# Centred products with tokens on the partitions, squares with row sums on ScalarE

## The reference, cut to what matters

```python
def _ln(x, g, b):
    mu = jnp.mean(x, axis=-1, keepdims=True)
    var = jnp.mean(jnp.square(x - mu), axis=-1, keepdims=True)
    return (x - mu) * jax.lax.rsqrt(var + EPS) * g + b

x1 = jnp.einsum('btd,hd->bth', x, sw1) + sb1
x2 = jnp.einsum('btd,hd->bth', x, sw2) + sb2
sh = _ln(jax.nn.silu(x1) * x2, s_ln_g, s_ln_b)       # 128 hidden features
shared_out = jnp.einsum('bth,dh->btd', sh, sw3) + sb3
...                                                   # a router and 8 experts, of the same form,
                                                      # for up to 512 routed tokens
final_out = shared_out.at[index_b, index_t].set(shared_moe_out + expert_moe_out)
```

## Time and profile before

| | us |
|---|---|
| median of three runs | 607.18 (607.03 to 607.24) |
| the profiled execution | 604.62 |
| its span | 602.0 |
| TensorE (PE) busy | 567.1, 94% of the span |
| VectorE (DVE) busy | 409.0, 68% |
| ScalarE (ACT) busy | 264.3, 44% |
| the squares L499, 8 operations | 4.8 |
| the variance matmuls L612, 64 passes | 8.1 |
| the centring matmuls L604, 16 | 4.8 |

### The profile page before, as it was taken

How to read it: one execution, slowest core, us unless ns; L and a number is a source line. 1 busy time by engine, 2 the same in 40 slices (tenths; PEclk the granted TensorE clock), 3 DMA queues, 4 the chain that set the end, 5 groups by cost and what they waited for, 6 DMA issues and landing times.

```text
span 602.0 us, 17044 instructions
## 1 busy us (share of the span) xinstructions
PE 567.1 (94%) x5093; PEld 499.6 (83%) x5094; DVE 409.0 (68%) x1092; ACT 264.3 (44%) x577; POOL 178.1 (30%) x529
## 2 busy tenths in 40 slices
PE   5999999999999999999999999999999979999770
PEld 4888888876899999999999999989999958667650
DVE  4969977757565868685677888756474735686560
ACT  6666667532444434344334343434343425464320
POOL 0350000000763444443424244443434002870000
PEclk9999999999999999999999999999999979999895
DMA  8812345001001232310000000000000001922130
GB/s 272 261 46 71 105 141 170 23 1 36 2 1 38 106 107 106 107 71 3 3 2 3 1 4 1 4 2 3 1 3 4 2 4 59 359 76 71 48 129 9
DMA packets 28482, 36.93 MB, mean 61 GB/s; under 512 B 4762, under 2 KB 24115, under 8 KB 28132
## 3 DMA queue, kind: packets, MB, share of 16 engines
q1 hardware_dynamic: 28292, 35.57, 18.0%
q0 software_dynamic: 96, 0.20, 0.1%
HBM read 27.30 MB, written 8.53 MB: 60 GB/s over the span
## 4 chain that ended last, share of the span: by engine, by line
PE 91%; DVE 3%; issue 1%; ACT 1%; DMA 1%; SPq 1%; POOL 0%; POOLq 0%; DVEq 0%
PE ps_out L1180 40%; PE ps_hidden L1152 39%; PE ps_hidden L592 3%; PE ps_hidden L641 1%; PE ps_out L612 1%; DMA W<-in_xT 1%; PE ps_turn L625 1%; PE ps_small L625 1%; PE ps_out L1223 1%; DVE X L782 1%; PE ps_out L604 1%; DVE hbuf L1327 0%; PE ps_hidden L625 0%; SPq L970 0%; DVE W L1311 0%
## 5 line engine op out<-in xcount | busy, mean ns | idle before, releaser
L1180 PE MATMUL ps_out<-hbuf,W 128*128 128x242 f16 (+2 forms) x2304 | 250.7, 269 | 0.7 <-DVE W L1311 0.6
L1180 PEld LDWEIGHTS ps_out<-hbuf,W 128*128 (+1 forms) x2304 | 223.8, 98 | 21.0 <-issue 1.3
L1721 POOL COPY xs<-X 128x88 f16 x352 | 128.4, 414 | 287.0 <-PE ps_hidden L1152 175.1
L1022 ACT ACTIVATE h<-ps_hidden,b 128x242 f32<-128x242 f32 (+1 forms) x384 | 155.8, 467 | 79.8 <-PE ps_hidden L1152 78.0
L1152 PE MATMUL ps_hidden<-xs,W 128*128 128x242 f16 x1536 | 164.2, 267 | 0.8 <-issue 0.8
L1152 PEld LDWEIGHTS ps_hidden<-xs,W 128*128 x1536 | 149.4, 98 | 10.8 <-issue 1.6
L1327 DVE TENSOR_TENSOR hbuf<-h,hbuf 128x484 f16<-128x484 f32 (+2 forms) x192 | 129.9, 676 | 7.4
L1608 DVE SCALAR_TENSOR_TENSOR acc<-ytmp,wrow,acc 128x44 f32 (+1 forms) x352 | 65.8, 259 | 92.4 <-ACT ytmp L1113 88.0
L1152 PE MATMUL ps_hidden<-X,W 128*128 128x256 f16 (+1 forms) x768 | 92.7, 283 | 10.3 <-DVE W L1311 6.1
L1325 DVE CAST hbuf<-h 128x484 f16<-128x484 f32 (+2 forms) x192 | 84.7, 441 | 22.4 <-ACT h L1022 21.2
L1152 PEld LDWEIGHTS ps_hidden<-X,W 128*128 128x128 f16 x768 | 76.6, 100 | 23.5 <-DVE W L1311 5.8
(11 more groups left out here) (291 smaller groups left out, 297.3 us busy)
## 6 DMA issues: line engine op xcount, KB each, us to landing
stage<-in_ew SPq DMA_DIRECT2D x16, 512.0 KB, 3.7
stage<-in_xR SPq DMA_DIRECT2D x8, 512.0 KB, 3.8
moved_rows<-stage SPq DMA_DIRECT2D x8, 512.0 KB, 2.6
X<-moved_rows SPq DMA_DIRECT2D x8, 512.0 KB, 9.2
out_rows<-X SPq DMA_DIRECT2D x16, 256.0 KB, 2.2
W<-in_xT SPq DMA_DIRECT2D x7, 512.0 KB, 9.2
W<-in_fw SPq DMA_DIRECT2D x1, 2304.0 KB, 12.5
W<-in_sw SPq DMA_DIRECT2D x4, 256.0 KB, 3.3
```

What stands on the lines that cost most here:

```text
L1022: i = nc.scalar.activation(h32[:, j, k * size:(k + 1) * size], ps1[j][:, k * size:(k + 1) * size], ACT.Gelu_apprx_tanh, bias=b1[:, bass.ds ...
L1180: mm = pe.matmul(out, w2(e, wp, hb, db), h, start=(n == 0), stop=(n == 3 * HB - 1))
L1721: i = nc.gpsimd.tensor_copy(xs[:, parity, :, j * SEG:(j + 1) * SEG], X[:, :, bass.ds(cols[j], SEG)])
```

## The change

`centre(k)` uses g's halves as the weights and `Cm` as the moving operand, group by group: 8 matmuls of 128 columns for 2 of 512. `Cm` is symmetric, so the result is the same matrix turned over: tokens on the partitions, features along the free dimension. `square(k)` becomes four operations of 128 columns, each with a second output, `accum_out`, the sum of its row: a token's sum of squares, in `sums2`. `variance` and its semaphore `var_mm` go away. `centre` alternates between the banks `psy[0]` and `psy[1]` and waits for the square of two chunks before. `roots` and `late_roots_in` wait for `sq_ready` and read `sums2` in place of `psy[1]`; `turn_hot`, which writes `psy[1]`, waits for the last square.

```diff
         qms = stf[:, 876:876 + 2 * MG]
+        sums2 = stf[:, 884:884 + NQ * MG]
         ohT = stf[0:FE, 1024:1024 + P]
...
         s_ready, g_made, g_hi, g_ready = sem("s_ready"), sem("g_made"), sem("g_hi"), sem("g_ready")
-        c_done, sq_ready, var_mm = sem("c_done"), sem("sq_ready"), sem("var_mm")
+        c_done, sq_ready = sem("c_done"), sem("sq_ready")
         var_taken, gvar_taken = sem("var_taken"), sem("gvar_taken")
...
                 act.wait_ge(c_done, k + 1)
-                if k >= 2:
-                    act.wait_ge(var_mm, k - 1)
-                nc.scalar.activation(sq[:, k % 2, :], psy[0], ACT.Square).then_inc(sq_ready, 1)
+                for n in range(MG):
+                    i = nc.scalar.activation(sq[:, k % 2, n * P:(n + 1) * P], psy[k % 2][:, n * P:(n + 1) * P],
+                                             ACT.Square, accum_out=sums2[:, k * MG + n:k * MG + n + 1])
+                i.then_inc(sq_ready, 1)
 
...
                 pe.wait_ge(g_ready, k + 1)
-                if k >= 1:
-                    pe.wait_ge(sq_ready, k)
-                else:
+                if k >= 2:
+                    pe.wait_ge(sq_ready, k - 1)
+                elif k == 0:
                     pe.wait_ge(late_done, 2)
-                for part in range(2):
-                    mm = pe.matmul(psy[0], Cm, ghl[:, k % GR, part, :], start=(part == 0), stop=(part == 1))
+                for n in range(MG):
+                    for part in range(2):
+                        mm = pe.matmul(psy[k % 2][:, n * P:(n + 1) * P], ghl[:, k % GR, part, n * P:(n + 1) * P], Cm,
+                                       start=(part == 0), stop=(part == 1))
                 mm.then_inc(c_done, 1)
-
-            def variance(k):
-                pe.wait_ge(sq_ready, k + 1)
-                if k >= 2:
-                    pe.wait_ge(var_taken, k // 2)
-                for n in range(MG):
-                    mm = pe.matmul(psy[1][:, k * MG + n:k * MG + n + 1], sq[:, k % 2, n * P:(n + 1) * P],
-                                   onesm[:, 0:1], start=True, stop=True)
-                mm.then_inc(var_mm, 1)
 
...
                 pe.wait_ge(hot2_ready, g + 1)
-                pe.wait_ge(var_taken, NQ // 2)
+                pe.wait_ge(sq_ready, NQ)
                 pe.transpose(psy[1][0:FE, 0:P], roh, ident[:, :]).then_inc(hot_turned, 1)
...
                 centre(k - 1)
-                if k >= 2:
-                    variance(k - 2)
                 if k >= 4:
...
             centre(NQ - 1)
-            variance(NQ - 2)
             second(4)
-            variance(NQ - 1)
             second(5)
...
             def roots(q):
-                dve.wait_ge(var_mm, 2 * q + 2)
+                dve.wait_ge(sq_ready, 2 * q + 2)
                 two = slice(2 * q * MG, (2 * q + 2) * MG)
-                nc.vector.tensor_scalar(tms, psy[1][:, two], 1.0 / FH, EPS, ALU.mult, ALU.add).then_inc(var_taken, 1)
+                nc.vector.tensor_scalar(tms, sums2[:, two], 1.0 / FH, EPS, ALU.mult, ALU.add).then_inc(var_taken, 1)
                 dve.wait_ge(var_taken, q + 1)
...
             def late_roots_in(q):
-                dve.wait_ge(var_mm, 2 * q + 2)
+                dve.wait_ge(sq_ready, 2 * q + 2)
                 two = slice(2 * q * MG, (2 * q + 2) * MG)
-                nc.vector.tensor_scalar(tms, psy[1][:, two], WS * WS / FH, EPS * WS * WS, ALU.mult,
+                nc.vector.tensor_scalar(tms, sums2[:, two], WS * WS / FH, EPS * WS * WS, ALU.mult,
                                         ALU.add).then_inc(var_taken, 1)
```

## The result

| | us |
|---|---|
| kernel before, median | 607.21 (607.03 to 607.63, 4 runs) |
| changed kernel, median | 603.39 (602.18 to 604.04, 4 runs) |
| ratio | 0.9934, 95% interval 0.9917 to 0.9951 |
| predicted | 604.7 (602.5 to 607.6) |

The changed kernel is 3.8 us faster; 2.5 was forecast. Measured again beside 23 runs of the kernel before, the ratio was 0.9925 (0.9897 to 0.9953).

A forecast was written before the change was run, and what follows sets the result against it. TensorE, busy 94% of 602.0 us, was taken as the bound. Of 4.74 us removed 0.90 stays; with 0.11 at its return and 1.50 in the tail, 2.5 less: 604.7 us, range 602.5 to 607.6.

The forecast's parts named there:

- 4.74 us taken out: Six groups of variance matmuls on TensorE's chain ahead of 560.77, 0.79 us each; all but 0.90 was to be taken back.
- S: ScalarE's queue time for one chunk's four squares with row sums; taken as 1.6 us, bounds 0.8 and 2.1, far end 3.0.
- The 0.95 for the high half of the input: ScalarE's queue time in each chunk's round for the half of the sum, 0.95 us of a 3.67 us round.
- the sum is nearly free: Rival: ScalarE's row sums add little, squares take 0.8 to 1.2 us a chunk; gain 3.7 to 4.5, 602.6 to 603.5; chance 0.15.
- three signs: Forecast wrong if squares' queue time is under 1.2 or over 2, TensorE shows no centring gaps, or the tail's low clock goes.
- main case: Forecast's own case: ScalarE's squares take 1.2 to 1.95 us a chunk, weight loads hidden; 603.4 to 606.0 us; chance 0.46.
- The walk: Stepping three engine queues in order with trace durations through the loop over k; TensorE's return behind the gap 1.01 us earlier.
- Waits at the centrings and at second(1): New TensorE waits in the loop: 0.57, 0.62, 0.62, 0.30, 0.44 and 1.12, together 3.67 us.
- the forecast 1.4: VectorE's inverse roots at chunk 3 were to start 1.4 us later than before, 534.21 against 532.79.
- Centring at 57 ns a matmul: Eight TensorE matmuls of 128 columns with weight loads hidden, 0.46 us a centring, +0.03 over before.
- The tail: From TensorE's return to the routed tokens' first centring: 4.61 us for 6.11, two variance groups gone, a gain of 1.50.
- The base: Whole kernel: profiled execution 604.62 becomes 602.1; the runs' median, 2.6 above the profiled one, gives 604.7 us.

The follow-up runs named there:

- squares made twice: Changed kernel with each chunk's four squares and row sums made a second time into spare buffers nobody reads; 605.2 us, ratio 0.9971 to the kernel before.
- split squares in the kernel before: Kernel before with only ScalarE's square split into four operations of 128 columns with unused row sums; 609.6 us, ratio 1.0034.
- without sums: Changed kernel with the squares' row sums taken out and the sums set to a constant 1; 602.9 us, ratio 0.9930 to the kernel before.
- wide centring: Changed kernel with the centring as before, two matmuls of 512 columns with the constant as weight; 603.1 us, ratio 0.9946 to the kernel before.
- filled pair: Changed kernel and kernel before, with 28 and 36 useless matmuls in TensorE's gap behind the last centring; 600.2 and 604.8 us.

## Why the prediction was right, and where it was off

- **That the 4.74 us taken out would mostly turn into waits at ScalarE and VectorE: right in kind, too large in size.** The term mis-sized is S, the square's queue time with its sums: 1.02 for 1.6. A square of 128 columns takes 0.16 of the queue (0.21 was taken) and the reading 0.09 (0.20 was taken, on the premise that it overlaps nothing; it overlaps both neighbours). The 0.95 for the high half of the input was also a little small: its row ends 0.09 us before the square starts, not after, and in the changed kernel it holds the queue for 0.99. The case that came is the rival *the sum is nearly free*, S 0.8 to 1.2, with 602.6 to 603.5; it had 0.15, and the measured 603.4 is in it. By two of the prediction's own three signs its main case was wrong: S is under 1.2, and ahead of the centrings of chunks 1 to 3 TensorE shows no gaps. The number fell inside the range because the range took in this rival, and that it is no further from 604.7 is partly luck: the mis-sized S made the forecast gain too small by 1.7 us, and the second low stretch, which nobody foresaw, takes up to 2.4 us from the real one.
- **The walk was right.** With S = 1.02 in place of 1.6 and nothing else altered it gives, shifted by 0.82 us so that chunk 1's first layer starts where the changed trace has it: first layer of chunk 5 at 535.19, `second(1)` 540.11, the last of `gfirst` 556.91, the return 563.36. The trace has 535.25, 540.15, 556.87, 563.35. The stretch is 2.81 us shorter than before; the walk for S = 1.6 had said 1.01. Since S was put in after it was known, this alone is a check of the walk and no forecast. The evidence that the queues are what limits here is that the same walk, before these runs were made, gave +3.5 for squares made twice (measured +3.61), 0 for split squares in the kernel before (+0.06) and -0.4 without sums (-0.34).
- **Waits at the centrings and at second(1).** Forecast 0.57 to 0.62 ahead of each of three centrings; a round is 3.10 to 3.12 us instead of 3.07, so 0.03 to 0.05 each. The inverse roots started at 533.35, 0.4 us later than before on a clock 0.74 behind, so not late at all; the forecast 1.4 was S again. What stays is 0.29 inside chunk 5's first layer (3.04 long in the timeline, the others 2.75; 0.30 was forecast), 0.29 ahead of chunk 4's centring (0.44) and 0.95 at `second(1)` (1.12), since VectorE has its 2.7 us of roots and its rows there whatever ScalarE does; with the squares made twice the last two are 0.27 and 0.95.
- **Centring at 57 ns a matmul: right.** 8 take 0.46 us (527.27 to 527.73). The Trainium skill, "TensorE: Matmul & The Clock Gate", section Back-to-back issue gap, has about 81 ns for this width in a stream of weight loads and matmuls; by an estimate from it, 8 x 81 ns, the row would be 0.65. The trace does not agree, and the measurement decides. The wide centring (0.43 for 0.46) is in line with it.
- **The tail: right.** 4.61 us forecast from return to centring with the clock low as long as before; 563.35 to 567.81 in the chain is 4.46, against 6.11 before: 1.65 gained for 1.50. (The table's 4.30 and 5.95 are the same stretch in the timeline, where a matmul's start is set 0.16 earlier.)
- **What was not foreseen:** the second low stretch, 574.2 to 581 us. The last second(7) takes 2.19 for 1.35 in it, and from the variance's first matmul to VectorE's last sum it is 12.8 us (571.68 to 584.49) for 10.4 before (575.40 to 585.82). It takes 2.4 us off a gain of 2.81 + 1.65 in this pair of profiles; with 0.74 that the changed profile is late already at the start of chunk 1's first layer, 0.60 of it from a low stretch at 490 us, 1.3 is left where the chains end.
- **The base.** The difference of 2.6 us between profile and median of the kernel before was carried over as a constant. It is not one: the changed kernel's profile took 603.60, near its median of 603.39. At an equal mean clock the two kernels differ by 4.3 us, and the filled pair by 4.0 to 4.6, with 2.81 and 1.68 in the two stretches; the walk with S = 1.02 and the tail as forecast make it 2.74 + 1.50 = 4.2.

## What to carry to other kernels

When work leaves the engine on the chain, write down the next engine's whole round and the slack in it: here ScalarE had 1.3 us, the change used 0.5 of it while TensorE's round shrank by 0.76, and the two ended within 0.05 us of each other; the cost of one unseen instruction decided how much of the saving came through. Walk the queues in order with durations of the trace, check the walk on the kernel as it is, and keep its inputs open, since a wrong input could here be replaced in one line. Where a program has gaps of some us on TensorE, compare runs at an equal mean granted clock (unless the change itself moves the clock, as the filling did: all six runs at 0.981 to 0.983), and look for work that can be moved into the gap: moving second(5) there brought about as much as the gap's whole filling.

## What the runs showed of the hardware

- A ScalarE square with a row sum is two instructions in the trace. The reading, 128 x 1, shows 0.19 to 0.23 us and costs 0.09 of the queue (1.02 for four squares with sums, 0.65 without).
- f16 matmuls of 128 columns, each with its own weights of 128 x 128, follow each other at 57 ns (0.46 us for 8).
- In eleven profiles of eleven with TensorE standing still for 2.2 to 4.3 us behind the last centring, the granted clock fell to 1.2 GHz within 1 us before or after its return. Useless matmuls in a gap of 3.5 us kept the clock at 2.4 GHz there and made the kernel 2.6 us faster.
- In 74 runs of one kernel the time spread over 7.5 us, in step with the mean granted clock from 0.982 to 0.973.
